# A graph network's row gathers, issued with at most two under way, and their landings counted by GpSimd in place of SyncE

## What is computed

```python
def _sage_layer(x, src, dst, inv_deg, W_self, W_neigh, b):
    agg = jax.ops.segment_sum(x[src], dst, num_segments=N_NODES)
    mean = agg * inv_deg[:, None]
    return x @ W_self + mean @ W_neigh + b

inv_deg = 1.0 / jnp.maximum(deg, 1.0)
h = jax.nn.relu(_sage_layer(features, src, dst, inv_deg, W0_self, W0_neigh, b0))
h = jax.nn.relu(_sage_layer(h, src, dst, inv_deg, W1_self, W1_neigh, b1))
h = _sage_layer(h, src, dst, inv_deg, W2_self, W2_neigh, b2)
# then: x = x + h; x = x + ffn(layernorm(x)), the ffn only for the half of the nodes with the highest router weight
```

## Time and profile before

| what | value |
|---|---|
| median of three runs | 5500.43 us |
| span of the profiled execution | 6674.4 us |
| that execution's own time outside its span | not given; the span is all the profile has |
| POOL busy | 3592.2 us, 54% of the span |
| PE busy | 4538.9 us, 68% |
| DVE busy | 2474.3 us, 37% |
| ACT busy | 1087.1 us, 16% |
| mean granted TensorE clock | 0.828 |
| gathers | 3780, mean 950 ns each on POOL |

### The profile page before, as it was taken

How to read it: one execution, slowest core, us unless ns; L and a number is a source line. 1 busy time by engine, 2 the same in 40 slices (tenths; PEclk the granted TensorE clock), 3 DMA queues, 4 the chain that set the end, 5 groups by cost and what they waited for, 6 DMA issues and landing times.

```text
span 6674.4 us, 106521 instructions
## 1 busy us (share of the span) xinstructions
PE 4538.9 (68%) x21019; PEld 2870.7 (43%) x21020; DVE 2474.3 (37%) x6444; ACT 1087.1 (16%) x2645; POOL 3592.2 (54%) x3790
## 2 busy tenths in 40 slices
PE   0465566657897775567776656664788988778884
PEld 0122223225775442244552222321566765556664
DVE  7244444443333332112222223332333344444446
ACT  6000111111112120000000000110111232223331
POOL 0544454435554665666666666656666555655551
PEclk9667777778998887788897777776889998899997
DMA  9334444445665554566665555554555654444445
GB/s 305 111 112 122 127 136 138 118 116 179 206 216 151 152 151 142 164 188 192 202 196 147 145 151 153 154 143 141 175 183 187 195 153 128 139 130 137 132 133 185
DMA packets 569508, 1057.15 MB, mean 158 GB/s; under 512 B 145479, under 2 KB 377875, under 8 KB 559827
## 3 DMA queue, kind: packets, MB, share of 16 engines
q0 software_dynamic: 241920, 743.42, 39.1%
q10 hardware_dynamic: 213078, 267.53, 11.7%
q1 hardware_dynamic: 114429, 45.18, 2.6%
HBM read 907.18 MB, written 148.63 MB: 158 GB/s over the span
## 4 chain that ended last, share of the span: by engine, by line
PE 31%; issue 28%; another core or an unknown queue 11%; DVEq 10%; DVE 9%; POOL 4%; ACT 3%; DMA 2%; ACTq 1%; SPq 0%; POOLq 0%
PE agg L953 10%; POOL gath L726 4%; PE y L1043 3%; PE agg L955 3%; PE hid L1033 2%; PE y L785 2%; PE lo L955 2%; PE hid L889 2%; PE lo L889 2%; PE count_ps L889 2%; DVEq L1315 2%; DVEq L1335 2%; DVEq L1450 1%; DVE onehot L1315 1%
## 5 line engine op out<-in xcount | busy, mean ns | idle before, releaser
L726 POOL DMA_INDIRECT gath<-table,idx_ring x3780 | 3590.7, 950 | 2947.8 <-issue 1280.6
L953 PE MATMUL agg<-gath,onehot 128*128 x4896 | 2055.3, 448 | 1173.0 <-issue 865.0
L953 PEld LDWEIGHTS agg<-gath,onehot 128*128 x4896 | 531.3, 109 | 1961.8 <-issue 1663.0
L955 PE MATMUL agg<-gath,onehot 128*128 x3264 | 993.6, 304 | 134.9 <-issue 129.0
L1315 DVE TENSOR_TENSOR onehot<-count_ps,dst_f 128x512 f32 x607 | 419.7, 691 | 1500.9 <-remote 706.0
L1322 DVE TENSOR_SCALAR onehot<-iota_row,window_base,dst_f 128x128 f16 x1324 | 342.4, 331 | 981.6 <-remote 344.2
L955 PE MATMUL lo<-gath,onehot 128*128 x1632 | 536.9, 329 | 36.8 <-issue 34.9
L1043 PE MATMUL y<-w_sb,hidT 128*128 128x256 f32 x1568 | 406.5, 417 | 115.0 <-ACT hidT L1947 92.8
L955 PEld LDWEIGHTS agg<-gath,onehot 128*128 x3264 | 343.2, 105 | 326.8 <-issue 240.6
L1033 PE MATMUL hid<-featT,w_gnn 128*128 128x128 f32 x3136 | 400.3, 285 | 58.1 <-issue 57.5
L1033 PEld LDWEIGHTS hid<-featT,w_gnn 128*128 128x128 f32 x3136 | 383.4, 200 | 80.1 <-issue 71.6
(11 more groups left out here) (204 smaller groups left out, 4412.0 us busy)
## 6 DMA issues: line engine op xcount, KB each, us to landing
dense<-counts_dram ACTq DMA_DIRECT2D x75, 1024.0 KB
gath<-table,idx_ring POOLq DMA_INDIRECT x3780
table<-split ACTq DMA_DIRECT2D x194, 192.0 KB
dense<-rows_f ACTq DMA_DIRECT2D x72, 512.0 KB
counts_dram<-dense ACTq DMA_DIRECT2D x16, 1600.0 KB, 8.4
rows_f<-y ACTq DMA_DIRECT2D x194, 128.0 KB
table<-gath ACTq DMA_DIRECT2D x24, 768.0 KB, 8.4
xb<-x ACTq DMA_DIRECT2D x97, 128.0 KB
```

The lines of the kernel that those rows point to most:

```text
L726: g.indirect_dma_start(gath[:, j, 0:PARTS * D], None, table[layer][:, :], bass.IndirectOffsetOnAxis(ap=idx_ring[:, h, i:i + 1], axis=0)).t ...
L953: mm(agg[p][:, 0:2 * D], oh, tile_rows[:, :, 0:2 * D], start=False, **flags)
L955: last = mm(low, oh, tile_rows[:, :, 2 * D:2 * D + lo_cols], start=False, **flags)
```

## The change

GpSimd itself now waits for landings. After it has issued gather `j` of a layer it waits until gather `j - 1` has landed, so that never more than two gathers are under way. The four landing semaphores now stand for the tile within its block (`landed[j % GROUP]`) and no longer for the block's place. Once the first gather of the next block is issued and the last one of this block has landed, GpSimd adds one to `rows_ready`. SyncE no longer hands landings on: it waits for `rows_ready` and loads the indices. The first turn of a layer is written out ahead of the loop, since its first gather has none before it; the limit `T0_MAX` on the turns skipped goes down by one for that.

```diff
-    T0_MAX = FULL_TURNS - 1
+    T0_MAX = FULL_TURNS - 2
-        landed = [sem(f"landed{q}") for q in range(RING_BLOCKS)]
+        landed = [sem(f"landed{k}") for k in range(GROUP)]
...
                     for h in range(2):
-                        for q in range(h * HALF_BLOCKS, (h + 1) * HALF_BLOCKS):
-                            if q < blocks:
-                                turns = FULL_TURNS + (q < LAST_BLOCKS)
-                                sp.wait_ge(landed[q], it * (16 * GROUP) + landed_base[q < LAST_BLOCKS])
-                            sp.sem_inc(rows_ready, 1)
-
+                        sp.wait_ge(rows_ready, it * RING_BLOCKS + (rows_base + (h + 1) * HALF_BLOCKS))
                         sp.dma_start(idx_ring[:, h, :],
...
+                def gather_landed(it, j):
+
+                    pool.wait_ge(landed[j % GROUP], it * (16 * RING_BLOCKS) + (landed_base + 16 * (j // GROUP + 1)))
+                    pool.sem_inc(pool_turn, 1)
+
-                def gather_turn(it, blocks):
+                def gather_turn(it, blocks, first=False):
...
-                                                     ).then_inc(landed[q], 16)
+                                                     ).then_inc(landed[j % GROUP], 16)
+                                if j or not first:
+                                    gather_landed(it, j - 1)
+                                if j % GROUP == 0 and (q or not first):
+                                    pool.sem_inc(rows_ready, 1)
...
-                with pool.Fori(t0 if layer else 0, last_turn) as it:
+                first_at = t0 if layer else 0
+                gather_turn(first_at, RING_BLOCKS, first=True)
+                with pool.Fori(first_at + 1, last_turn) as it:
                     gather_turn(it, RING_BLOCKS)
                 gather_turn(last_turn, LAST_BLOCKS)
+                gather_landed(last_turn, LAST_BLOCKS * GROUP - 1)
+                pool.sem_inc(rows_ready, 1 + RING_BLOCKS - LAST_BLOCKS)
```

More of the change, by code:

```diff
@@ L644, in _, with load_turn @@
             for layer in range(LAYERS):
-                def relay_turn(it, blocks):
+                def load_turn(it):
                     turn_at = nc.s_assert_within(
@@ L658, in relay_turn @@
                                      ).then_inc(idx_loaded[h], 16)
-                landed_base = [turns_left * (16 * GROUP * layer) + 16 * GROUP * (layer * more + 1) if layer else 16 * GROUP
-                               for more in range(2)]
+                rows_base = sp.snap(turns_left * (RING_BLOCKS * layer) + RING_BLOCKS * layer) if layer else 0
                 with sp.Fori(t0 if layer else 0, last_turn) as it:
-                    relay_turn(it, RING_BLOCKS)
-                relay_turn(last_turn, LAST_BLOCKS)
+                    load_turn(it)
+                load_turn(last_turn)
             for h in range(2):
@@ L715, in _ @@
                         pool.wait_ge(slots_stored[k], 16 * (1 + BATCHES // 4 + (k < 2)))
-                def gather_turn(it, blocks):
+                landed_base = turns_left * (16 * RING_BLOCKS * layer) + 16 * LAST_BLOCKS * layer if layer else 0
+                def gather_landed(it, j):
+                    pool.wait_ge(landed[j % GROUP], it * (16 * RING_BLOCKS) + (landed_base + 16 * (j // GROUP + 1)))
+                    pool.sem_inc(pool_turn, 1)
+                def gather_turn(it, blocks, first=False):
                     for h in range(2):
```

## The result

The changed kernel takes 8277.88 us (median of four runs, 8266.45 to 8283.58), beside 5500.84 us for the kernel before in the same series. The ratio is 1.5047, 95% interval 1.5024 to 1.5070. The forecast was 8020 us, with 7250 to 8650 as the range.

A forecast was written before the change was run, and what follows sets the result against it. The prediction took POOL's gather issue rate as the bound. Capped at two, 1260 gathers a layer at 2.03 us give 2558 us; three layers plus start, end and layer changes make 8020 us, range 7250 to 8650.

The forecast's parts named there:

- The gather stream bounds the kernel before, within 8%: POOL's gather issue at 1.25 us each, 5075 us in all, sets the unprofiled kernel's pace; its median is 5500.43 us.
- The landing, 3.05 us from the start: Time from a gather's start on POOL to the engine that waits for it: 3.05 us, later under load.
- The wake, 0.8 us, and 0.05 for added instructions in two gathers: POOL's sequencer, once released from a wait, starts the next gather 0.8 us later; added semaphore and register instructions take 0.05.
- The late landings, 0.08 us a gather: Landings delayed by other queues' traffic raise a gather from 1.95 us to at most 2.10; the middle, 2.03, was taken.
- The sum: Whole kernel: 157 + 3 x 2558 + 59 + 134 = 8024 us, carried over unscaled from the profile as 8020 us.
- The waits for free places all but go: POOL's waits for ring places nearly vanish because the ring is rarely full; some of layer 0's stay.
- SyncE's hand-over, the count, the index loads: nothing: Moving the block count from SyncE to POOL and the index loads' timing cost or gain nothing under the slower stream.
- rival A: Faster: loads and stores get through sooner and PE no longer waits for SyncE; at best 58 us, 5440 us; 3%.
- B: No change: the cap binds a little and 425 us of slack absorbs it; needs a landing near 1.9 us; 2%.
- C: Slower by much less: landings come sooner, at 2.61 us, so 1.73 us a gather and 6890 us; 9%.
- D: Slower still: half of the landings late, mean 4.1 us, so 2.49 us a gather and 9760 us; 6%.
- theory L: A capped gather costs landing plus wake, divided by the number under way, and never less than POOL's own 1.25 us.

The follow-up runs named there:

- the second profile: The kernel before, unchanged, profiled again: span 5502.7 us, time 5504.55 us; the first profile's span was 6674.4 us.
- at three and four: The changed kernel with three or four gathers under way instead of two, GpSimd counting: 6099.44 us (1.1095 of the kernel before) and 5681.85 us (1.0329).

## Why the prediction was right

- *The gather stream bounds the kernel before, within 8%.* Right as a sum over the layers, and plainly so for layer 1, at 1.29 us a gather in the second profile. Layer 0 stood at 1.54, and in layer 2, at 1.31, PE's feed-forward products are as much of the chain (30%) as POOL's gathers (20%). What I gave as the reason for the long span, that the other engines are slower under the profiler, was wrong: the second profile has the length of the runs. Carrying the sum over unscaled was right all the same: the changed kernel's span, 8278.9, is its run's time.
- *The landing, 3.05 us from the start.* Right for a quiet landing: 3.07 and 3.06 in the rows shown, and 3.08 in the median of all 3780, POOL's own answer in it.
- *The wake, 0.8 us, and 0.05 for added instructions in two gathers.* Right for the plain round, 0.78 to 0.80 us, but too small as a mean, which is 0.93. Where the next gather opens a block the wake is 0.97 us in the median, and where it opens a turn 1.34: there POOL's loop (line 740) and its waits for indices and a place stand in it as well, for example from 4012.96 to 4014.32 in the chain, 1.36 us. The loop had no price in the sum.
- *The late landings, 0.08 us a gather.* Right in kind, too small in size. From the start of a gather to the start of the next but one is its landing and the wake; the mean landing is 3.28 us, so late ones cost (3.28 - 3.05) / 2 = 0.12 us a gather. I took less because fewer gathers would queue behind each other. In the changed kernel's chain one late landing stands between two quiet ones:

```profile
4009.88 3.08 DMA gath<-table,idx_ring
...
4014.32 6.43 DMA gath<-table,idx_ring
...
4021.55 2.98 DMA gath<-table,idx_ring
```

  The landings that are late are late behind other transfers. By the packet records, 2965 of the 3780 gathers had under 64 KB of other queues' packets in their first 3 us, and 18 of these were more than 1 us later than the quiet 3.05; of the 416 with 200 KB or more, 184 did. Leaving out the dense windows' loads of two layers brought 150 us.
- *The sum.* With the measured ends (156 + 125 + 45 = 326) a gather costs (8278 - 326) / 3780 = 2.10 us, the upper end of my own bounds, where I had 2.03. Late landings and wakes share what was missing, each with 0.04 us a gather or some 140 us; the ends are 24 us shorter than the 350 that I put in. That makes up the 258 us between forecast and result. In the sum no mechanism was wrong; two small terms were, both to the same side.
- *The waits for free places all but go.* Right in the main: PE's releases are 451 us of POOL's idle time in the second profile of the kernel before (the 710 of the earlier trace rows is from the first, longer one), and 137 us now. The signs named ahead came too, but for layer 0, which at 2719 us is longer than the 2500 to 2700 given. What ends POOL's idle time now (us, times):

```profile
  DMA gath<-table,idx_ring: 3120.4, 1918
  issue: 1159.4, 1783
  DMA table<-gath: 154.1, 1
  PE agg L964: 100.4, 61
  PE lo L964: 36.6, 17
```

- *SyncE's hand-over, the count, the index loads: nothing.* Right: with SyncE counting 8282.53 against 8277.88. The bound on rival A was read from the first profile, though: in the second one PE's wait for SyncE is no 58 us beside the start but most of its waiting:

```profile
L953 PE MATMUL agg<-gath,onehot 128*128 x4522 | 1780.8, 425 | 803.9 <-SPq L654 665.2 <-DVE onehot L1315 92.2 <-issue 38.3
```

  That wait is for the gathers, which SyncE only reports. Under the cap, moving the report was worth nothing; moving it without a cap was not tried.
- *The rivals.* A and B needed a landing below 1.9 us; the shortest of 3780 is 2.94. C's early landings did not come, and neither did D's half of all landings late: 357 of 3780 are more than half a microsecond above the quiet landing. The price that the Trainium skill's page "DMA: Bandwidth & Descriptors" gives (section "Anatomy of one DMA — SWDGE (gpsimd) path") makes an estimate of 2.45 us for such a gather. The trace has 3.08 us from the gather's start, or 2.14 when POOL's own 0.94 is taken off, so it agrees from neither end; the prediction's remark that it agrees with POOL's 0.95 us put first was wrong, since that makes 3.40. For two thirds fewer bytes the same estimate takes off 0.30 us, where the traces show 0.53.

The shortfall of theory L at three and four has late landings in it again. At four, POOL's own pace takes 4 x 1.25 = 5.0 us for four gathers; by these numbers a landing later than 5.0 - 0.8 = 4.2 us holds POOL up. No trace has gathers less than 1.24 us apart, so the time is not made up afterwards. In that kernel's trace POOL waits 339 us for landings, 402 times. Without a cap the ring has room for sixteen gathers, and POOL goes on issuing. Of the 184 us at four, the loads of layers 1 and 2 are about 97. By the stretches of its trace, layer 0, which had its loads in every run, is 23 us longer than in the kernel before (1958.5 against 1935.2); what the rest is was not tried.

None of the capped versions beats the kernel before. The time falls with the cap (15629, 8278, 6099, 5682 us for one to four) towards 5500 without one.

## What to carry to other kernels

A cap on transfers under way puts the completion into the issuing loop: the pace is (landing + wake) / cap, and it costs nothing only while that is well below what the issuing engine needs by itself. Read the landing from the row of whoever waits for it today, and the wake from a place where the issuing engine has really stood idle: here it is 0.8 us after a wait, where two gathers without one have 0.30 us between them. Price the rounds that carry more instructions, such as the end of a loop, by themselves. Leave room for the late landings, since a capped stream cannot make them up: here a cap of four should have been free by the quiet numbers and cost 3%.

## What was not expected of the hardware

- The shortest wake does not vary: 0.76 us of issue after the semaphore in the kernels with one and with two under way, however long the wait was, after 3.07 us as after 6.43. What varies is what else the sequencer has to do in the round.
- A quiet landing is 3.0 to 3.1 us with one and with two under way; a second gather's packets do not delay the first one's. Only 1.04 us of it lie between the gather's first packet and its last; 1.64 us pass before them and 0.37 after. What delays a landing is other queues' traffic: 221 of the 3780 in the changed kernel are more than 1 us late, 123 of them more than 3.
- TensorE's granted clock fell with its work, from a mean of 0.888 in the second profile of the kernel before to 0.767, and 0.63 with one gather under way; the matmuls on gathered rows took 489 ns in place of 425. What that costs was not tried; POOL's waits that PE ended are 137 us in all.
